# Layer 0's mixture of experts with folded biases, its residual terms prepared by GpSimd, and its weight products moved into the attention

## The reference

```python
y1 = _ln(x + _mha(x, in_proj_w, in_proj_b, out_proj_w, out_proj_b), ln1_g, ln1_b)
y2 = _ln(y1 + _moe(y1, wg, w1, b1, w2, b2), ln2_g, ln2_b)
# _moe: top-1 of 8 experts by softmax(y1 @ wg), capacity 1024 tokens each, no activation:
h = disp @ w1 + b1 ; y = h @ w2 + b2 ; out = gate_val * y (0 past the capacity)
# and in the model: x = x + tanh(g_ffn[0]) * y2(_layernorm(x))
```

## Time and profile before

| | us |
|---|---|
| time, median of 3 runs | 2786.68 (2780.58 to 2786.93) |
| span of the profiled execution | 2897.0 |
| l0_attention in that span | 62.7 to 341.4 |
| l0_route | 341.4 to 359.3 |
| l0_experts | 359.3 to 553.1 |
| all the rest (layer 0's first part, layers 1 to 3), worked out | 2406.6 |

### The profile page before, as it was taken

How to read it: one execution, slowest core, us unless ns; L and a number is a source line. 1 busy time by engine, 2 the same in 40 slices (tenths; PEclk the granted TensorE clock), 3 DMA queues, 4 the chain that set the end, 5 groups by cost and what they waited for, 6 DMA issues and landing times. The chain is left out here.

```text
span 2897.0 us, 59646 instructions
## 1 busy us (share of the span) xinstructions
PE 2275.3 (79%) x20218; PEld 1760.5 (61%) x20218; DVE 1835.0 (63%) x5797; ACT 1197.1 (41%) x2400; POOL 1173.9 (41%) x1364
## 2 busy tenths in 40 slices
PE   4888799687729999995887786089974888879776
PEld 1455522286628888883655554089972665558665
DVE  7688667688746666664885676210014677864588
ACT  1566334244313333333654453034423555655332
POOL 4455268523451111114334444523335555435611
PEclk6788899788759999996997787589995899989898
DMA  7200011332010000003101100122221111100001
GB/s 207 93 19 20 29 44 45 103 108 61 22 55 24 24 24 24 24 16 109 29 25 34 30 27 23 43 64 71 71 80 39 32 35 35 27 2 10 7 26 33
DMA packets 153438, 129.78 MB, mean 45 GB/s; under 512 B 18996, under 2 KB 131390, under 8 KB 152392
## 3 DMA queue, kind: packets, MB, share of 16 engines
q1 hardware_dynamic: 130120, 92.31, 10.7%
q0 software_dynamic: 12288, 25.45, 3.0%
q10 hardware_dynamic: 10752, 8.39, 0.9%
HBM read 79.99 MB, written 46.10 MB: 44 GB/s over the span
## 5 line engine op out<-in xcount | busy, mean ns | idle before, releaser
L1826 PE MATMUL scores<-l1ffn_x_t,l1ffn_w 128*128 128x256 f32 x888 | 230.5, 383 | 0.0
L1791 POOL COPY l1ffn_w<-l_w_ahead 128x1032 f32 x74 | 75.2, 1047 | 347.3 <-DVE l1ffn_hid L1899 339.6
L1914 DVE SCALAR_TENSOR_TENSOR l1ffn_acc<-bank,l1ffn_xs,l1ffn_acc 128x128 f32<-128x128 f32 x518 | 157.9, 347 | 71.5 <-PE bank L1838 66.2
L2649 DVE TENSOR_REDUCE l_top<-scores 128x16 f32<-128x1024 f32 x128 | 155.5, 1215 | 61.3 <-DMA l1mix_ctx<-in_ctx 35.7
L2580 ACT ACTIVATE l_probs_t<-bank 128x512 f32<-128x512 f32 x256 | 140.6, 596 | 124.8 <-PE bank L237 109.0
L1838 PEld LDWEIGHTS bank<-l_w_ahead,l1ffn_hid 128*128 128x128 f32 x1184 | 178.3, 191 | 15.4 <-issue 0.3
L1838 PE MATMUL bank<-l_w_ahead,l1ffn_hid 128*128 x1184 | 179.6, 274 | 0.1
L3038 DVE COPY l2ffn_y<-bank 128x512 f32<-128x512 f32 x34 | 23.5, 692 | 241.8 <-PE bank L2943 241.8
L2509 PE MATMUL bank<-l_v_blocks,l_probs_t 128*64 128x18 f32 x4096 | 155.9, 220 | 21.8 <-issue 20.2
L237 PEld LDWEIGHTS bank<-ident,l_probs 128*128 128x128 f32 x1024 | 135.2, 158 | 59.1 <-issue 44.2
L2509 PEld LDWEIGHTS bank<-l_v_blocks,l_probs_t 128*64 128x64 f32 x4096 | 144.6, 150 | 37.9 <-issue 35.1
(11 more groups left out here) (497 smaller groups left out, 5848.3 us busy)
## 6 DMA issues: line engine op xcount, KB each, us to landing
l2ffn_xs<-scratch_l_in SPq DMA_DIRECT2D x136, 64.0 KB, 1.8
scratch_l_out<-l2ffn_y SPq DMA_DIRECT2D x34, 256.0 KB, 2.3
x_all<-scratch_x SPq DMA_DIRECT2D x32, 256.0 KB, 4.2
l_ctx_t<-in_ctx_t SPq DMA_DIRECT2D x32, 256.0 KB
l_w_ahead<-in_l_w SPq DMA_DIRECT2D x3, 2048.0 KB, 15.1
l1ffn_xs<-scratch_l_in SPq DMA_DIRECT2D x37, 136.0 KB, 2.2
scratch_l_out<-l1ffn_acc SPq DMA_DIRECT2D x37, 128.0 KB, 1.8
x_all<-in_x SPq DMA_DIRECT2D x16, 256.0 KB, 5.7
```

The costliest lines, as they stand in the source:

```text
L1826: mm = pe.matmul(bank[1 + m % HB][:, part * TP:(part + 1) * TP], w13[:, j % WR, k, c:c + P], x_t[:, j % 2], start=True, stop=True)
L1914: v.scalar_tensor_tensor(out=acc[:, j % 2, t, :], in0=bank[5 + p % 2][:, c:c + D], scalar=xs[:, j % RING, t, D + e:D + e + 1], in1=acc[:, ...
L2649: v.tensor_reduce(peak, raw, AX.X, ALU.max).then_inc(topped, 1)
```

## The change

- **Experts.** The bias products of L951 are gone, with the splitting of b12 into three parts, the three DMAs that lay them out and the GpSimd `memset` for them. The transposed row that the experts multiply is now the normalized row z without gain and bias, plus one. The weights are changed to fit: affine = diag(ln1_g) + (ln1_b - ln1_g) / 128 (every element of row k of the latter is that of feature k), so that (z + 1) @ affine gives z * g + b by way of the sum of z being 0, and w12 = affine' @ w12_raw + b12 / 128. `move_x` is gone, as x already holds tanh(g) * ln2_b. The two first DMAs of y1 are issued first, and ln2_g after them.
- **Route.** w1 @ w2, b1 @ w2 and the loads of the constants are gone from it. TensorE makes four products of 128x512 with two passes each (affine by w12_raw, and `even` by b12_blocks). The sum of the exponentials stands before the wait for `based`. The last addition on VectorE (L845) is gone.
- **Attention.** VectorE's `norm_y` is one `tensor_scalar` a tile, four a group, in the place of eight instructions, and waits for the root first. ScalarE adds one in its copy of the transposed row. GpSimd gets three operations of 128x512 a group: x + tanh(g) * ln2_b in slots with s = 0, and y1 * ln1_g and + ln1_b, four groups late, in s = 1 and s = 2. At the start two more DMAs are waited for (nine in the place of seven), and VectorE makes `affine`, a column of ones and the scaled ln2_b ahead of the first normalization. In slots 65 to 72 TensorE makes b1 @ w2 (four products a slot, two passes each), in slots 73 to 80 w1 @ w2 (four products a slot, one expert each); ScalarE copies the results in slots 73, 77 and 81, GpSimd makes b12_blocks in slot 75. b1, b2 and the two constants are loaded behind w1_t and w2.

The diff, cut to its core:

```diff
@@ l0_attention
+        ln_cols, ln2_b, one = ph.sb("ln_cols", [P, 2]), ph.sb("ln2_b", [P, D]), ph.sb("one", [P, 1])
...
-                                  (ln_g, "l0_ln1_g"), (ln_b, "l0_ln1_b"), (wg, "l0_wg")):
+                                  (ln_g, "l0_ln1_g"), (ln_b, "l0_ln1_b"), (wg, "l0_wg"), (ln_cols, "l0_ln1_cols"),
+                                  (ln2_b, "l0_ln2_b")):
...
                         ahead.start(sp)
+                        sp.dma_start(b1[:, :, :], dram["l0_b1"]).then_inc(b1_in, DMA)
+                        sp.dma_start(b2[:, :], dram["l0_b2"]).then_inc(b1_in, DMA)
+                        route_in.start(sp)
...
+                def whole_y1(g):
+                    pool.wait_ge(y1_scaled, g + 1)
+                    pool.tensor_tensor(y1_all[...group g...], y1_all[...], ln_b[...], ALU.add).then_inc(y1_whole, 1)
+                def scale_y1(g):
+                    pool.wait_ge(y1_turned, g + 1)
+                    pool.tensor_tensor(y1_all[...group g...], y1_all[...], ln_g[...], ALU.mult).then_inc(y1_scaled, 1)
+                def shift_x(g):
+                    pool.wait_ge(z_done, (g + 1) * G)
+                    pool.tensor_tensor(x_all[...group g...], x_all[...], ln2_b[...], ALU.add).then_inc(x_plus, 1)
...
                 def slot(n, i, s):                                  # GpSimd
                     tile(n - 1, normalize)
+                    if s == 0:
+                        group(i, shift_x)
                     if s == 1:
                         group(i + 2, lambda g: root(0, g))
+                        group(i - 4, scale_y1)
                     if s == 2:
                         group(i + 2, add_bias)
+                        group(i - 4, whole_y1)
                     if s == 3:
                         group(i - 2, lambda g: root(1, g))
+                    if n == BIAS + 10:
+                        spread_b12()
...
+                def merge_bias(n):                                  # TensorE
+                    if n == BIAS:
+                        ahead.wait(pe)
+                        pe.wait_ge(b1_spread, 1)
+                        pe.wait_ge(exped, TILES * H)
+                    for k in range(4 * (n - BIAS), 4 * (n - BIAS) + 4):
+                        mm = pe.matmul(bank[2][0:L0_E, 0:D], b1_wide[:, k * L0_E:(k + 1) * L0_E], w2[...],
+                                       start=(k == 0), stop=(k == L0_E * C0 - 1))
...
+                def merge(n):
+                    e = n - MERGE
+                    for c in range(C0):
+                        mm = pe.matmul(bank[e // 4][:, e % 4 * D:(e % 4 + 1) * D], w1_t[:, e, c, :], w2[:, e, c, :],
+                                       start=(c == 0), stop=(c == C0 - 1))
+                    mm.then_inc(merged, 1)
...
                     if s == 3:
                         group(i - 3, turn_y1)
+                    if BIAS <= n < BIAS + 8:
+                        merge_bias(n)
+                    if MERGE <= n < MERGE + 8:
+                        merge(n)
...
-                    act.activation(y1_t[:, g % 2], bank[7][:, :], ACT.Identity).then_inc(y1_t_done, 1)
+                    act.activation(y1_t[:, g % 2], bank[7][:, :], ACT.Identity, bias=one[:, 0:1]).then_inc(y1_t_done, 1)
...
                 def norm_y(g):                                      # VectorE
-                    v.wait_ge(var_done[1], (g + 1) * G)
-                    for t in range(G):
-                        v.scalar_tensor_tensor(out=gained[...], in0=res[...], scalar=mv[...], in1=ln_g[:, :],
-                                               op0=ALU.subtract, op1=ALU.mult).then_inc(gained_done, 1)
                     v.wait_ge(rstd_done[1], g + 1)
                     for t in range(G):
-                        v.wait_ge(gained_done, g * G + t + 1)
-                        v.scalar_tensor_tensor(out=y1_all[...], in0=gained[...], scalar=rstd[...], in1=ln_b[:, :],
-                                               op0=ALU.mult, op1=ALU.add).then_inc(y1_done, 1)
+                        v.tensor_scalar(y1_all[:, g * G + t, :], res[:, g % 2, t, :], mv[:, 1, g % 2, t, 0:1],
+                                        rstd[:, 1, g % 2, t:t + 1], ALU.subtract, ALU.mult).then_inc(y1_done, 1)
@@ l0_route
-                for e in range(E):
-                    for c in range(C):
-                        mm = pe.matmul(bank[1 + e // 4][...], w1_t[:, e, c, :], w2[:, e, c, :], ...)
+                for half in range(2):
+                    e4 = slice(half * 4, half * 4 + 4)
+                    pe.matmul(bank[1 + half][:, :], affine[:, :], w12_raw[:, e4, :]..., start=True, stop=False)
+                    pe.matmul(bank[1 + half][:, :], even[:, :], b12_blocks[:, e4, :]..., start=False, stop=True)
+                route_in.wait(pe)
                 pe.wait_ge(done, 7)
                 pe.matmul(bank[0][:, 0:E], later[:, :], count[:, :], start=True, stop=True).then_inc(based, 1)
-                for k in range(E * C):
-                    mm = pe.matmul(bank[3][0:E, 0:D], b1_wide[:, k * E:(k + 1) * E], w2[:, k // C, k % C, :], ...)
@@ l0_experts
                         pe.matmul(out, tile, w12[...],
-                                  start=True, stop=False)
-                        pe.matmul(out, ones[:, :], b_rows[:, half * HALF * D:(half + 1) * HALF * D],
-                                  start=False, stop=True).then_inc(made, 1)
+                                  start=True, stop=True).then_inc(made, 1)
...
-                        move_x(g)
...
-                                               scalar=ln.rstd[:, t:t + 1], in1=x_plus[:, g % 2, t, :],
+                                               scalar=ln.rstd[:, t:t + 1], in1=x_all[:, g * G + t, :],
```

More of the change, by code:

```diff
@@ L362, in _, with l0_attention @@
                     mix(g)
-def l0_attention(chip, y1_all, logits, ahead):
+def l0_attention(chip, y1_all, logits, ahead, fold_in, route_in):
     nc, dram, x_all, bank, ident = chip.nc, chip.dram, chip.x_all, chip.bank, chip.ident
@@ L380, in l0_attention @@
     RP, RT, RR, RV = 4, 3, 5, 3
+    C0 = L0_FF // P
+    BIAS, MERGE = 65, 73
+    w1_t, w2 = ahead.tensors
     with Phase(chip, "l0att") as ph:
@@ L733, in slot @@
                         group(i - 2, add_residual)
+                    if n == BIAS - 1:
+                        spread_b1()
                 x_stats(0)
@@ L740, in _, with l0_route @@
                 over_slots(slot)
-def l0_route(chip, logits, weight, ahead, w12, b12):
-    nc, dram, bank = chip.nc, chip.dram, chip.bank
-    E, C = L0_E, L0_FF // P
+def l0_route(chip, logits, weight, route_in, fold_in, w12):
+    nc, bank = chip.nc, chip.bank
+    E = L0_E
     with Phase(chip, "l0route") as ph:
-        w1_t, w2 = ahead.tensors
-        b1, b1_wide, b2 = ph.sb("b1", [P, E, C]), ph.sb("b1_wide", [P, E * C * E + 8]), ph.sb("b2", [E, D])
-        b1_in, b1_zero, b1_spread, merged, merged_out = (ph.sem("b1_in"), ph.sem("b1_zero"), ph.sem("b1_spread"),
-                                                         ph.sem("merged"), ph.sem("merged_out"))
-        first, later = ph.sb("first", [P, E]), ph.sb("later", [P, P])
+        first, later = route_in.tensors
+        affine, even, w12_raw, b12_blocks = fold_in
+        folded, w12_done = ph.sem("folded"), ph.sem("w12")
         best, total = ph.sb("best", [P, TILES]), ph.sb("total", [P, TILES])
@@ L964, in _ @@
             def _(v):
[L965 to L973 removed]
+                v.wait_ge(w_in, DMA)
                 v.tensor_scalar(ln_g[:, :], ln_g[:, :], tanh_g, None, ALU.mult).then_inc(affine, 1)
[L975 to L976 removed]
+                v.wait_ge(affine, 1)
                 def accumulate(p, experts):
@@ L3460, in build @@
             ahead = Ahead(chip, l0, "l0", w1_t=[P, L0_E, L0_FF // P, D], w2=[P, L0_E, L0_FF // P, D])
-            l0_attention(chip, y1_all, logits, ahead)
             w12 = l0.enter_context(nc.sbuf_tensor("l0_w12", [P, L0_E, D], F32))
-            b12 = l0.enter_context(nc.sbuf_tensor("l0_b12", [L0_E, D], F32))
-            l0_route(chip, logits, weight, ahead, w12, b12)
-            l0_experts(chip, y1_all, weight, w12, b12)
+            fold_in = [l0.enter_context(nc.sbuf_tensor(f"l0_{what}", shape, F32))
+                       for what, shape in (("affine", [P, P]), ("even", [L0_E, P]), ("w12_raw", [P, L0_E, D]),
+                                           ("b12_blocks", [L0_E, L0_E, D]))]
+            route_in = Ahead(chip, l0, "l0r", first=[P, L0_E], later=[P, P])
+            l0_attention(chip, y1_all, logits, ahead, fold_in, route_in)
+            l0_route(chip, logits, weight, route_in, fold_in, w12)
+            l0_experts(chip, y1_all, weight, w12)
         pairs = Pairs(chip, ctx)
@@ L3513, in layouts @@
         "l0_ln1_b": rows(i["L0_ffn_ln1_b"]),
+        "l0r_first": rows(np.arange(L0_E, 0, -1, dtype=np.float32)),
+        "l0_ln1_cols": np.stack([i["L0_ffn_ln1_g"], i["L0_ffn_ln1_b"]], axis=1),
+        "l0r_later": (s[:, None] < s[None, :]).astype(np.float32),
```

158 lines of the change are left out of this document (81 added, 77 removed).

## The result

| | time, median (range) | ratio to before |
|---|---|---|
| before | 2783.16 us (2779.98 to 2786.93) | |
| after | 2765.64 us (2759.20 to 2775.51) | 0.9939 [0.9925, 0.9954] |

The change is worth -17.5 us, or 0.6%, and the interval of the ratio leaves out 1. The kernel is faster, and the time lies inside the range of the prediction, but the gain is half of the forecast -33.8. The profiled execution of after has a span of 2760.6 us, near its median; the one of before was some 110 us longer than its timed runs.

The account below looks back on a forecast made before the run. TensorE alone was taken to bound the experts, TensorE the route, no engine the attention's steady part. The terms 2.0 + 0 + 5.6 - 7.2 - 1.3 - 32.9 = -33.8 took 2786.7 to 2753 us, range 2742 to 2770.

Parts of the forecast that it names:

- Attention, start: Attention's start: two more loads waited for and VectorE's extra preparation move z from 68.18 to 70.2, +2.0 us.
- Attention, steady part: Attention's repeating groups: VectorE's halved norm_y and GpSimd's added 3.8 us a group change nothing, 0 (-2 to +6).
- third rival: Attention: GpSimd becomes the bound, its three added operations costing 61 us; total +27, 2814 us; chance 0.06.
- Drain: End of the attention: 128 merging passes on TensorE at 0.110 us each, 14.1 us, lengthen it by +5.6.
- which a TensorE without gaps should be granted: Attention's drain: TensorE's own 10.49 us at clock 0.78 counted as about 8.2 at full clock.
- Route: Route: from 19.1 to 11.9 us, VectorE's chain remaining and the new products mostly under it; -7.2 (-7.7 to -5).
- Experts, start and steady part: Experts: -1.3 at the start (earlier y1 load, fewer bias products) and -32.9 in the steady part.
- the price of a group: Experts' steady part: a group of four tiles at 8.9 us, the middle between 8.48 and 9.4, from 10.98.
- upper end of 9.4: Experts' steady part: group time if GpSimd without idle time meets VectorE's whole run of 2.5 us; -25.0 us.
- lower end: Experts' steady part: TensorE's 8.48 us a group, eight halves of 1.06; -39.6 us.
- second rival: Experts: GpSimd and VectorE in turn bound them at 9.4 us a group; total -25.9, 2761 us; chance 0.25.
- Sum: Whole kernel: 2.0 + 0 + 5.6 - 7.2 - 1.3 - 32.9 = -33.8 us.

Follow-up runs that it names:

- x5: The kernel after without GpSimd's three new operations a group in the attention; 2762.89 us, ratio 0.9939.
- x4: The kernel after with VectorE's copy of b1 (spread_b1) moved from slot 64 to slot 40; 2756.97 us, ratio 0.9915.
- x7: x4 with GpSimd's two y1 steps, in the last four groups, waiting for the next group's norm_y; 2751.94 us, ratio 0.9893.
- x6: x4 with all 128 merging passes (b1 @ w2, w1 @ w2) moved back into the route; 2769.80 us, ratio 0.9960.
- x1: The kernel before with only the experts' bias products (L951) left out; 2772.21 us, ratio 0.9971.
- x3: The kernel after with GpSimd's additions in the experts cut to one column; 2742.24 us, ratio 0.9860.
- x2: The kernel after with a bfloat16 bias product of zeros put back after each half tile; 2798.24 us, ratio 1.0055.
- x8: The kernel after with ScalarE normalizing in the experts and VectorE multiplying and adding for whole groups; 2777.16 us, ratio 0.9980.
- x11: x8's experts reordered, with x7's drain, three buffers for acc, and add_to_x a group later; 2734.49 us, ratio 0.9839.

## Why the prediction was right in sign and half in size

- **Attention, start, +2.0:** z moved from 68.18 to 70.48, +2.3 (1.8 from the phase's own start). Right.
- **Attention, steady part, 0:** -3.0 in these two traces, which is inside the scatter of the steady part, so no change is shown. Right in kind: x5 shows that GpSimd's additions cost nothing there beyond that scatter, which refutes the third rival with its 61 us. But one of my reasons was wrong. I let VectorE save four of eight passes a group; it saved none (47.0 to 47.7 us). It did not matter, as VectorE has idle time there.
- **Drain, +5.6, bounds +4 to +12:** +16.4. The step that failed is "which a TensorE without gaps should be granted". It had two gaps, 3.58 and 1.97 us, and behind them passes at a mean granted clock of 0.58 (322 to 324) and 0.64 (the last 40). The first gap comes from one instruction that I did not cost at all, `spread_b1`, a copy in VectorE's queue behind a wait for the root and `norm_y`. By the length of the drain x4 takes away 8.1 us and x7 2.6, and what is left, 28.9 - 23.3 = +5.6, is the term that I had worked out: in x7 TensorE is busy without a gap from 318.0 to 340.9, as I had assumed. The +5.4 that x6 puts on the merging passes fits too.
- **Route, -7.2:** -8.0 against x1 and -7.5 against the profile of before. Right, with the folding products hidden.
- **Experts, start and steady part, -34.2:** -26.5. The failed step is the price of a group, 8.9 us: it is 9.77, over the upper end of 9.4 and over the 9.5 from which on I had called myself wrong. I took TensorE's 8.48 as the lower end, but without the bias products its passes are faster, and it would need under 7.3 (two times 3.60 to 3.67). And I let GpSimd pay for the meeting with VectorE, as in the row of 2.40 us. Once TensorE no longer gave both of them slack, VectorE paid: 8.20 (x3) became 9.77. By the prediction's own sum, 126 halves of 9.77 / 8 = 1.221 us, the steady part would have given -19.2 only, and the sum, with all other terms as forecast, -20.1. What made up for it lies at the stage's ends, which I had at -1.3. From the stage's start to GpSimd's root of the first group (L204 in both kernels) it is 24.3 us before and 17.9 after, -6.4: 0.9 of it is the earlier load, as forecast, and the rest the first tiles, where VectorE has no layer norm yet and keeps up with the faster TensorE (it still stands 1.27 and 0.87 us waiting for it there). The fourteen beats from there to the root of the fifteenth group give 17.2 (154.0 to 136.8), and the one to the root of the last group, behind which no further tiles come, gives 2.8 (9.97 to 7.22). So -26.5 is near the -26.3 of my second rival by luck: its group of 9.4 and its reason, a GpSimd that waits, are both wrong.
- **Sum:** the drain took 10.8 us more than forecast and the experts 7.7; the route gave 0.8 more, and the traces' 3.0 in the attention's steady part is scatter. The time lies inside the range, whose upper end allowed for the second rival with a slow drain; but the two misses together, 18.5 us, are more than the gain that was measured. The bias product alone was worth 9.6 us (x1), not the 32 that its share of the beat promised.

The Trainium skill ("SBUF — State Buffer", section "Who interferes with whom") has the exclusive lock and says that the order of issue, not the shape, decides who is blocked. The traces agree that the shape does not decide: the same two operations met at 2.40 us for GpSimd and 1.14 for VectorE in before and x2, and at 0.84 and 1.96 in after. And they agree on the order at the start of VectorE's run: in 15 groups of each of after, x1 and x4 an addition had been issued before the run and was still going, and VectorE was held; in before and x2 none had been, and GpSimd was held. Why GpSimd's later additions of the same run also get in between (443.12 in after) the rows don't show. The Trainium skill also names, in the same section, one-input operations in a two-port mode as contenders, and its "VectorE: DVE Perf Modes" (section "Mode 2×_2P — use both read ports for one tensor") counts a float32 `tensor_scalar` within SBUF among them. That is the new `norm_y`: four passes of 1.11 us alone (x5, x7) took 3.88 and 4.72 in after's drain beside GpSimd's products and additions of y1. I had read the rule for the two-input passes and left this one out.

## What to carry to other kernels

When the bounding work is removed, price the next engine by what it needs without slack: an engine that was idle a quarter of the time may have been spared collisions by that idle time, and either of the two may then be the one that pays: here it was VectorE, in whose run of passes an addition of GpSimd was already under way. Before work is moved into another queue's waits, list every instruction that feeds it, also the tiny ones, and look what each is queued behind: here a copy of 0.18 us cost over 7 us. An operation moved to an engine with idle time is only worth it if the chain back is buffered as deep as it is long (x8 to x11: the same operations gave +11.5, -1.4 and then -14 to -16 us more with one buffer and a later place).

## What the hardware showed unexpectedly

- A float32 pass of 512 columns takes 0.43 us when nothing stands between such passes, and 0.53 when a bfloat16 product stands after each pair (x2 puts it back: 1.06 us a pair). The product of 0.31 us costs 0.51 a half.
- A run of passes of VectorE can keep GpSimd out to its end, not for one instruction: two columns took 2.47 us (x3), the length of eight passes and more. There, as in before and x2, no addition of GpSimd was under way when the run began, or only one with 0.02 us left. Where one was (after), the later ones got in between the passes at 0.84 and 0.85 us, and the run took 3.75 us in the place of 2.18.
- A float32 `tensor_scalar` of 128x128 with two scalars per partition takes 0.26 us from start to start in VectorE's queue (1.11 for four), no less than a `scalar_tensor_tensor` (1.13), and it is held up beside GpSimd: 804 ns on average in after, 517 once GpSimd's three operations a group are gone (x5).
